# A graph attention block on one core: output projection and residual from two f16 parts, and a reordered first stage

## The chip, the cores and the metric

The kernel runs on one core of one Trainium2 chip. The metric is the time of one execution in device microseconds, lower is better; the runs' median is what is compared. One further execution was profiled, and its trace gives the views and rows below.

## The reference

Inputs are x (2048 rows of 256), an adjacency matrix adj of 2048 x 2048 integers, a node mask, h_target (2048 x 256) and the weights of one attention layer with 8 heads of 32 (H, HD) and of a feed-forward of 4 x 256:

```
h  = relu(layernorm(x))
hs = layer_norm(h; ln1) masked;  ht = layer_norm(h_target; ln1) masked
q, k, v = ht @ Wq + bq, hs @ Wk + bk, hs @ Wv + bv          # q also / sqrt(32)
logits  = q k^T per head, -1e30 where edge_mask (adj) is 0
ctx     = softmax(logits) v
ht      = ht + where(tmask, ctx @ Wo + bo, 0)               # output projection and residual
ht      = layer_norm(ht; ln2) masked
out     = x + ht + gelu(ht @ W1) @ W2
```

## The kernel before

Five engines run programs written out by hand, and semaphores order them. The name `mm` at line 469 issues nearly every matrix product, so products are told apart by their tiles.

**First stage.** Rows of x and of h_target are normed and turned (`turn_rows`), and `features` (ACT) writes them with features in partitions: sources into nT, targets of block 0 into nTq. `project(g)` makes queries (g = 0) and keys of the four source blocks (g = 1 to 4) from f32 operands, `values(i)` the values of two source tiles; `high_parts`, `low_parts`, `high_values` and `low_values` split the results into an f16 high part and the rest. SyncE (SP) copies the parts of keys and queries into place for each pair of heads (`place_k`, `place_q`, line 377), as soon as they are staged. `early_scores(e, i)` are unmasked scores of 128 targets by 1024 sources, from which DVE takes row maxima (`maxima`, L1203); the first eight pairs are one head. `shift_row` then turns the negated maxima into one more row of the queries, and five scores of the main loop (AHEAD) are made before it begins. POOL norms sources (L1416), multiplies them with the node mask (`drop_sources`, L1431), and makes two masks (L1436). `UNREAD` products (20 of them) are read by nobody.

**Main loop.** There are 32 units, a head (8) of a block of 512 targets (4): unit u is block k = u // 8 and r = u % 8. A unit has 16 steps s, one for each tile of 128 sources. In a step PE makes the masked scores of five steps ahead (4 mask products and one of 512 columns) into one of two banks, half a pair of early scores for two units ahead, and the context of the current tile: 8 products of 65 columns from the f16 or bf16 high part of the exponential and its f16 low part. ACT makes the exponential (L888). The low part, `prob_lo`, is a subtraction: of 16 in a unit DVE makes 4 (L1211) and POOL 12 (L1412), in units with r = 5 three and 13. Eight slots hold the parts. ACT copies the context out once per unit (L910).

Extra work stands at steps given by tables of (r, s): for block k + 1 `turn_targets` and `query_features` (QT_AT), `queries` (QP_AT), in f32; for block k - 1 sums of the context's halves (POOL, SUM_AT), norms (ACT, NORM_AT, four steps of two small copies each), `turn_context` and `context_T` (CT_AT), and the out rows (WO_AT). Two weights of the feed-forward are split in eight pieces, high parts on ACT (`weight_high`, step 6, L972), low parts on POOL (`weight_low`, step 12, L1453).

**The out row** (`out_row`, PE): for 128 targets the turned context times Wo in f32, and the turned target features times an identity in f32, both added up in a half of the bank aux:

```python
for c in range(DC):
    mm(dst, cT[:, c, t * P:(t + 1) * P], wo[:, c, :], c == 0, False, skip_group_check=True)
for c in range(DC):
    last = mm(dst[:, c * P:(c + 1) * P], nTq[:, k % 2, c, t * P:(t + 1) * P], ident32[:, :], False,
              c == DC - 1, skip_group_check=True)
```

Blocks 0 to 2 have theirs at r = 2, steps 11 and 12, and r = 3, steps 1 and 2 of the next block. `rows_out` (ACT) copies them out two by two.

**End.** After the loop the feed-forward runs block by block from f16 parts (`up_products`, `gelus` and their split, `down_products`), with the last block's context turned after f = 5 and 7 of block 0 and its four out rows after f = 2 and 4 of block 1.

## Time and profile before

| | |
|---|---|
| runs | 692.8 us median of 3 (689.97, 692.81, 692.8) |
| the profiled execution | 694.41 us, its span 692.6 us, mean granted clock 0.993 |
| busy, share of the span | PE 95%, DVE 82%, POOL 76%, ACT 70% |
| instructions | 20346, of them 8346 matrix products |
| DMA | 36.23 MB, mean 52 GB/s |
| parts of the span | first stage to 70.9 us, main loop to 593.3, the rest to 692.6 |

A product's busy time on PE contains its latency, and products overlap, so PE's work is read from start to start. The chain of work that ended last goes back only through the last few per cent of the span, so it says little here; the stages were read from the timeline, from the waits and from stretches of the span.

### The profile page before, as it was taken

Reading aid. Unit: us, or ns where it says so; the run is one execution under the profiler, and the core shown is the slowest. Engines: PE = TensorE matmul, PEld = TensorE weight load, DVE = VectorE, ACT = ScalarE, POOL = GpSimd, SP = SyncE. Lnnn points to the kernel's source line nnn. Section 1 sums busy time; section 2 is a strip of 40 time slices with the busy share of each in tenths; the row PEclk is TensorE's granted clock in tenths of the full one; section 3 lists DMA queues with packets and bytes.
Section 4 is the critical chain, followed back from the end, with each engine's and each line's share of the span. In section 5 each row is a group of like instructions: output and inputs, shape, how many; then the busy total and the mean of one; then the engine's idle time right before and its main releaser. Section 6 shows DMA issues by size and latency. Waiting matters only on the chain. (4 is left out here: it accounts for less than half of the span.)

```text
span 692.6 us, 20346 instructions
## 1 busy us (share of the span) xinstructions
PE 657.6 (95%) x8346; PEld 473.0 (68%) x8346; DVE 569.2 (82%) x946; ACT 484.0 (70%) x932; POOL 524.2 (76%) x488
## 2 busy tenths in 40 slices
PE   4898999999999999999999999999999899899998
PEld 4465667766776777677767766777777567557767
DVE  5987899989999879999997798989868888575661
ACT  4865668766778858677787686778866788867550
POOL 3574889889999957899998678999977777471430
PEclk9998999999999999999999999999999999999999
DMA  8735501113001011220011112012000000000001
GB/s 296 258 80 153 177 31 36 59 63 108 2 2 34 2 62 63 58 82 2 2 33 33 62 33 78 17 51 74 2 2 2 2 3 2 1 1 32 24 17 54
DMA packets 20797, 36.23 MB, mean 52 GB/s; under 512 B 2752, under 2 KB 13280, under 8 KB 20704
## 3 DMA queue, kind: packets, MB, share of 16 engines
q1 hardware_dynamic: 20704, 34.92, 16.2%
q8 instruction: 66, 1.08, 0.6%
q14 instruction: 27, 0.22, 0.1%
HBM read 26.49 MB, written 2.10 MB: 41 GB/s over the span
## 5 line engine op out<-in xcount | busy, mean ns | idle before, releaser
L1412 POOL TENSOR_TENSOR prob_lo<-prob 128x512 f16<-128x512 f32 x382 | 437.1, 1169 | 74.1 <-ACT prob L888 73.2
L888 ACT ACTIVATE prob<-score 128x512 f32<-128x512 f32 x512 | 304.1, 597 | 135.8 <-PE score L469 128.3
L469 PE MATMUL score<-nidentb,mask_nat 128*128 128x128 bf16 x2048 | 199.1, 220 | 4.1 <-ACT qT L905 1.9
L469 PE MATMUL early<-kT,qT 96*128 96x512 f16 x512 | 192.9, 382 | 10.5 <-DVE half_max L1203 10.1
L469 PEld LDWEIGHTS ctx<-v_sb,prob 128*128 128x128 bf16 x2048 | 159.0, 98 | 60.2 <-ACT raw L910 12.6
L469 PE MATMUL score<-qT,kT 97*128 97x512 f16 x512 | 196.3, 383 | 0.0
L1203 DVE CUSTOM_DVE_ANT_0 early<-early,mask_nat,half_max 128x1024 f32<-128x1024 f32 x128 | 163.6, 1287 | 38.0 <-PE early L469 36.0
L469 PE MATMUL ctx<-v_sb,prob 128*128 128x65 f16 x2048 | 191.4, 193 | 2.3 <-ACT raw L910 1.8
L469 PE MATMUL ctx<-v_sb,prob_lo 128*128 128x65 f16 x2048 | 190.4, 193 | 0.0
L469 PEld LDWEIGHTS ctx<-v_sb,prob_lo 128*128 128x128 f16 x2048 | 142.6, 97 | 49.9 <-issue 4.0
L1203 DVE CUSTOM_DVE_ANT_0 early<-early,mask_nat 128x1024 f32<-128x1024 f32 x128 | 157.1, 1229 | 22.5 <-PE early L469 20.8
L1211 DVE TENSOR_TENSOR prob_lo<-prob 128x512 f16<-128x512 f32 x130 | 127.8, 984 | 4.1 <-ACT prob L888 4.0
L469 PEld LDWEIGHTS score<-nidentb,mask_nat 128*128 128x128 bf16 x2048 | 122.6, 98 | 8.9 <-ACT prob L888 3.2
L469 PEld LDWEIGHTS early<-kT,qT 96*128 96x128 f16 x512 | 50.6, 99 | 21.4 <-DVE half_max L1203 18.4
L469 PEld LDWEIGHTS score<-qT,kT 97*128 97x128 f16 x512 | 50.3, 98 | 0.0
L1509 POOL TENSOR_TENSOR mask_nat<-mask_nat,tgt 128x256 f32<-128x256 f32 x16 | 15.3, 965 | 44.9 <-DVE mask_nat L1355 44.9
L1341 DVE TENSOR_TENSOR kT<-qT,kT 128x512 f16<-128x512 f32 x32 | 27.3, 859 | 20.5 <-ACT kT L1081 20.5
L469 PE MATMUL early<-w_f,kT 128*128 128x256 f16 x384 | 42.7, 273 | 0.7 <-DVE adj_in L1364 0.7
L469 PEld LDWEIGHTS early<-w_f,kT 128*128 128x128 f16 x384 | 37.4, 98 | 6.1 <-DVE adj_in L1364 1.2
L1203 DVE DVE_READ_ACCUMULATOR2_ANT half_max<- 128x1 f32 x256 | 35.5, 139 | 0.0
L1077 ACT ACTIVATE qT<-score 128x512 f32<-128x512 f32 x32 | 19.0, 593 | 19.4 <-PE score L469 14.9
L1191 DVE TENSOR_SCALAR mask_nat<-adj_in 128x1024 bf16<-128x1024 int32 x26 | 26.3, 1016 | 0.0
(167 smaller groups left out, 623.2 us busy)
## 6 DMA issues: line engine op xcount, KB each, us to landing
adj_in<-in_adj SPq DMA_DIRECT2D x26, 512.0 KB, 4.0
qT<-q_stage SPq DMA_DIRECT2D x48, 64.0 KB, 2.0
kT<-mask_nat SPq DMA_DIRECT2D x48, 64.0 KB, 2.0
raw<-in_x SPq DMA_DIRECT2D x4, 512.0 KB, 5.6
tgt<-in_L_gnn_h_target SPq DMA_DIRECT2D x4, 512.0 KB, 11.6
prob<-in_adj SPq DMA_DIRECT2D x4, 512.0 KB, 10.4
nT<-in_L_gnn_W SPq DMA_DIRECT2D x2, 1024.0 KB, 6.6
mask_nat<-in_x SPq DMA_DIRECT2D x1, 2048.0 KB, 8.3
```

Source lines behind the costliest of these rows:

```text
L469: return nc.tensor.matmul(dst, w, m, start=start, stop=stop, **more)
L888: nc.scalar.activation(prob[:, n % SLOTS, :], score[n % 2][:, :], ACT.Exp).then_inc(exp_done, 1)
L1077: nc.scalar.activation(gelu[:, f % 2, :], up[f % 2][:, :], ACT.Gelu_apprx_tanh).then_inc(gelu_ready, 1)
L1191: nc.vector.tensor_scalar(mask_half(k, i), adj_home(k, i), 0.0, BIG, ALU.is_equal, ALU.mult).then_inc(mask_dve, 1)
L1203: nc.vector.tensor_tensor_reduce(out=early[e % 2][:, :], in0=early[e % 2][:, :], in1=mask_nat[:, k % 2, t, half * HALF:(half + 1) * HALF], ...
L1211: nc.vector.tensor_tensor(prob_lo[:, n % SLOTS, :], prob[:, n % SLOTS, :], prob_hi(n % SLOTS), ALU.subtract).then_inc(lo_sem["dve"], 1)
L1341: nc.vector.tensor_tensor(g_lo[:, k % 2, f, :], gelu[:, f % 2, :], g_hi[:, k % 2, f, :], ALU.subtract).then_inc(g_lo_done, 1)
L1412: nc.gpsimd.tensor_tensor(prob_lo[:, n % SLOTS, :], prob[:, n % SLOTS, :], prob_hi(n % SLOTS), ALU.subtract).then_inc(lo_sem["pool"], 1)
L1509: nc.gpsimd.tensor_tensor(xin[:, n - 1, :], xin[:, n - 1, :], tgt[:, n - 1, :], ALU.add).then_inc(r_done, 1)
```

## The change

The out rows take f16 parts: context, Wo and target features are each a high and a low f16 part, Wo needs three products where there was one in f32 (high x high, high x low, low x high), and the residual two. ACT makes the high parts as copies to f16: Wo once (unit 3, step 2), the features of a block at the steps T_HIGH, the context one step after its copy out. POOL makes the low parts as f32 minus f16 to f16: `output_low`, `feature_low`, `context_low`, at its steps WO_LOW, T_LOW and C_LOW. The parts of the context lie in cT, those of the features in nTq; the f32 forms lie in q_stage (context), in the second half of nTq (features of block 0) and in cT (features of blocks 1 to 3). The first pair of out rows moves from step 11 to 12. In the first stage 24 unread products come in (UNREAD_LATER), `project(2)` and `project(3)` are halved around `turn_rows`, two pairs of early scores come ahead of `project(4)`, `values(2)` to `values(7)` follow the early scores of the same number, `shift_row(0)` goes ahead of the tenth pair, and the orders of ACT, DVE and POOL are written anew.

```diff
-WIDE, UNREAD = 64, 20
+WIDE, UNREAD, UNREAD_LATER = 64, 20, 24
...
-WO_AT = {(2, 11): 0, (3, 1): 1}
+WO_AT = {(2, 12): 0, (3, 1): 1}
...
+T_HIGH = {0: [(3, 7), (3, 9)], 1: [(4, 6), (4, 8)]}
+T_LOW = {0: [(3, 12), (3, 15)], 1: [(4, 11), (4, 14)]}
+C_LOW = [(2, 10), (2, 12)]
+WO_HIGH, WO_LOW = (3, 2), (4, 5)
...
+        t_full = [nTq[:, 1, :, :], cT[:, :, :], cT[:, :, :], cT[:, :, :]]
+
+        t_parts = [nTq[:, i, :, :].rearrange("p c t -> p (c t)").bitcast(F16).rearrange("p (r c t) -> p r c t", r=2, c=DC)
+                   for i in range(2)]
+        c_full = [cnorm[:, :, c * P:(c + 1) * P] for c in range(DC)]
+        c_parts = cT[:, :, :].rearrange("p c t -> p (c t)").bitcast(F16).rearrange("p (r c t) -> p r c t", r=2, c=DC)
...
+                    if t == 0:
+                        pe.wait_ge(wo_lo, 1)
+                        pe.wait_ge(c_lo, DC * (k + 1))
+                        pe.wait_ge(t_lo, DC * (k + 1))
                     dst = aux[:, t % 2 * D:(t % 2 + 1) * D]
+                    part = slice(t * P, (t + 1) * P)
                     for c in range(DC):
-                        mm(dst, cT[:, c, t * P:(t + 1) * P], wo[:, c, :], c == 0, False, skip_group_check=True)
+                        for a, w in ((0, 0), (0, 1), (1, 0)):
+                            mm(dst, c_parts[:, a, c, part], wo_parts[:, w, c, :], c == a == w == 0, False, skip_group_check=True)
                     for c in range(DC):
-                        last = mm(dst[:, c * P:(c + 1) * P], nTq[:, k % 2, c, t * P:(t + 1) * P], ident32[:, :], False,
-                                  c == DC - 1, skip_group_check=True)
+                        for a in range(2):
+                            last = mm(dst[:, c * P:(c + 1) * P], t_parts[k % 2][:, a, c, part], ident16[:, :], False,
+                                      c == DC - 1 and a == 1, skip_group_check=True)
...
                 values(0)
+                for i in range(UNREAD_LATER):
+                    mm(early[1][:, TB:TB + P], identb[:, :], identb[:, :], True, True)
+                project(2, (0,))
                 turn_rows(3)
-                project(2)
+                project(2, (1,))
                 values(1)
+                project(3, (0,))
                 turn_rows(4)
-                project(3)
-                values(2)
-                for i in range(2):
-                    early_scores(0, i)
-                project(4)
-                for e in range(1, RAMP + 2):
+                project(3, (1,))
+                for e in range(2):
                     for i in range(2):
                         early_scores(e, i)
-                    if e + 2 < NT // 2:
-                        values(e + 2)
-                shift_row(0)
+                project(4)
+                for e in range(2, RAMP + 2):
+                    if e == RAMP + 1:
+                        shift_row(0)
+                    for i in range(2):
+                        early_scores(e, i)
+                    if e < NT // 2:
+                        values(e)
...
+                    nc.scalar.activation(c_full[c], aux[:, :].rearrange("p (t q) -> p t q", t=TT), ACT.Copy).then_inc(aux_done, 1)
...
+                def context_high(k, c):
+                    act.wait_ge(aux_done, AUX["cT", k, c] + 1)
+                    if c == 0 and k + 1 < NTB:
+
+                        act.wait_ge(t_lo, DC * (k + 2))
+                    nc.scalar.activation(c_parts[:, 0, c, :].rearrange("p (t q) -> p t q", t=TT), c_full[c], ACT.Copy).then_inc(c_hi, 1)
...
+                    affine(t_full[k][:, c, :], aux[:, :], LN1_G[:, c:c + 1], RES_B[:, c:c + 1]).then_inc(aux_done, 1)
...
+                def feature_high(k, c):
+                    if k == 0:
+                        act.wait_ge(nT_done, c + 1)
+                    else:
+                        act.wait_ge(aux_done, AUX["qT", k, c] + 1)
+                    if c == 0:
...
+                    nc.scalar.activation(t_parts[k % 2][:, 0, c, :], t_full[k][:, c, :], ACT.Copy).then_inc(t_hi, 1)
+
+                def output_high():
+                    nc.scalar.activation(wo_parts[:, 0, :, :], wo[:, :, :], ACT.Copy).then_inc(wo_hi, 1)
...
+                features(2)
                 deviation(2)
...
-                features(2)
+                high_values(0)
                 deviation(3)
-                last_sources()
-                high_values(0)
...
+                last_sources()
...
                 high_parts(3)
+                high_parts(4)
+                high_values(2)
+                feature_sum(0)
+                feature_sum(1)
+                for i in range(3, 6):
+                    high_values(i)
                 for k in range(1, 3):
                     target_deviation(k)
                 nc.scalar.activation(warm_c, eps_c, ACT.Exp).then_inc(act_link, 1)
-                high_values(2)
-                high_parts(4)
-                feature_sum(0)
-                high_values(3)
-                high_values(4)
-                feature_sum(1)
-                for i in range(5, NT // 2):
-                    high_values(i)
+                high_values(6)
                 negated(0)
                 row_out(0)
+                high_values(7)
...
+                        if k == 0 and (r, s) in T_HIGH[0]:
+                            feature_high(0, T_HIGH[0].index((r, s)))
+                        if k + 1 < NTB and (r, s) in T_HIGH[1]:
+                            feature_high(k + 1, T_HIGH[1].index((r, s)))
+                        if (u, s) == WO_HIGH:
+                            output_high()
...
+                            if (r, s - 2) in CT_AT:
+                                context_high(k - 1, CT_AT[r, s - 2])
...
+                        context_high(NTB - 1, f // 2 - 2)
...
+                low_parts(0)
...
-                low_parts(0)
                 low_parts(1)
                 low_values(0)
+                make_mask(0, 0)
+                low_parts(2)
+                for i in range(1, TT):
+                    make_mask(0, i)
+                low_values(1)
+                low_parts(3)
+                maxima(0)
+                maxima(1)
+                low_parts(4)
+                maxima(2)
+                low_values(2)
+                make_mask(0, 4)
+                maxima(3)
+                make_mask(0, 5)
                 target_stats(1)
-                low_parts(2)
+                maxima(4)
                 target_stats(2)
-                low_values(1)
-                for i in range(2):
-                    make_mask(0, i)
-                low_parts(3)
-                for i in range(2, TT):
-                    make_mask(0, i)
-                maxima(0)
-                low_values(2)
-                low_parts(4)
-                maxima(1)
-                make_mask(0, 4)
-                maxima(2)
-                make_mask(0, 5)
-                for e in range(3, RAMP + 1):
+                for e in range(5, RAMP + 2):
                     maxima(e)
-                for e in range(RAMP + 1, RAMP + FILL):
+                for e in range(RAMP + 2, RAMP + FILL):
                     maxima(e)
...
+                def output_low():
+                    pool.wait_ge(wo_hi, 1)
+                    nc.gpsimd.tensor_tensor(wo_parts[:, 1, :, :], wo[:, :, :], wo_parts[:, 0, :, :], ALU.subtract).then_inc(wo_lo, 1)
+
...
+                    parts = t_parts[k % 2]
+                    nc.gpsimd.tensor_tensor(parts[:, 1, c, :], t_full[k][:, c, :], parts[:, 0, c, :], ALU.subtract).then_inc(t_lo, 1)
...
+                def context_low(k, c):
+                    pool.wait_ge(c_hi, DC * k + c + 1)
+                    hi, lo = (c_parts[:, i, c, :].rearrange("p (t q) -> p t q", t=TT) for i in range(2))
+                    nc.gpsimd.tensor_tensor(lo, c_full[c], hi, ALU.subtract).then_inc(c_lo, 1)
...
                 source_norm(1)
+                drop_sources(1)
                 source_norm(2)
-                drop_sources(1)
...
+                        if k == 0 and (r, m) in T_LOW[0]:
+                            feature_low(0, T_LOW[0].index((r, m)))
+                        if k + 1 < NTB and (r, m) in T_LOW[1]:
+                            feature_low(k + 1, T_LOW[1].index((r, m)))
+                        if k > 0 and (r, m) in C_LOW:
+                            context_low(k - 1, C_LOW.index((r, m)))
+                        if (u, m) == WO_LOW:
+                            output_low()
...
+                for c in range(DC):
+                    context_low(NTB - 1, c)
```

How it moves instructions, on PE in the first stage from the values of the first tiles to the first scores (mask_nat and raw are sources, cT holds the weights of keys and values here, kT and qT make the early scores). Before:

```order
L469 MATMUL early<-cT,nT 128x256 x4
L483 MATMUL score<-ident,raw 128x128 x8
L469 MATMUL ctx<-nT,cT 128x512 x2
L469 MATMUL aux<-nT,cT 128x512 x2
L469 MATMUL early<-cT,nT 128x256 x4
L483 MATMUL score<-ident,raw 128x128 x8
L469 MATMUL ctx<-nT,cT 128x512 x2
L469 MATMUL aux<-nT,cT 128x512 x2
L469 MATMUL score<-cT,nT 128x256 x4
L469 MATMUL early<-kT,qT 128x512 x2
L469 MATMUL ctx<-nT,cT 128x512 x2
L469 MATMUL aux<-nT,cT 128x512 x2
```

And now:

```order
L485 MATMUL early<-cT,nT 128x256 x4
L485 MATMUL early<-identb 128x128 x24
L485 MATMUL ctx<-nT,cT 128x512 x2
L499 MATMUL score<-ident,raw 128x128 x8
L485 MATMUL aux<-nT,cT 128x512 x2
L485 MATMUL early<-cT,nT 128x256 x4
L485 MATMUL ctx<-nT,cT 128x512 x2
L499 MATMUL score<-ident,raw 128x128 x8
L485 MATMUL aux<-nT,cT 128x512 x2
L485 MATMUL early<-kT,qT 128x512 x4
L485 MATMUL ctx<-nT,cT 128x512 x2
L485 MATMUL aux<-nT,cT 128x512 x2
```

The 24 products on identb are new, the two key projections after them are cut in halves of two products, and four early products stand ahead of the last key projection.

On POOL from the loop's start to the middle of block 0 (prob_lo is the loop's own subtraction, w_f the weights' low part). Before:

```order
L1412 TENSOR_TENSOR prob_lo<-prob 128x512 x60
L1453 TENSOR_TENSOR w_f<-nT,w_f 128x512
L1412 TENSOR_TENSOR prob_lo<-prob 128x512 x13
L1453 TENSOR_TENSOR w_f<-nT,w_f 128x512
L1412 TENSOR_TENSOR prob_lo<-prob 128x512 x12
L1453 TENSOR_TENSOR w_f<-nT,w_f 128x512
L1412 TENSOR_TENSOR prob_lo<-prob 128x512 x12
L1453 TENSOR_TENSOR w_f<-nT,w_f 128x512
```

And now:

```order
L1474 TENSOR_TENSOR prob_lo<-prob 128x512 x48
L1524 TENSOR_TENSOR nTq<-nTq 128x512
L1474 TENSOR_TENSOR prob_lo<-prob 128x512 x2
L1524 TENSOR_TENSOR nTq<-nTq 128x512
L1474 TENSOR_TENSOR prob_lo<-prob 128x512 x5
L1519 TENSOR_TENSOR wo_parts<-wo,wo_parts 128x512
L1474 TENSOR_TENSOR prob_lo<-prob 128x512 x4
L1524 TENSOR_TENSOR nTq<-cT,nTq 128x512
L1474 TENSOR_TENSOR prob_lo<-prob 128x512
L1515 TENSOR_TENSOR w_f<-nT,w_f 128x512
L1474 TENSOR_TENSOR prob_lo<-prob 128x512
L1524 TENSOR_TENSOR nTq<-cT,nTq 128x512
```

Five subtractions of 128x512 come in among them: the features' of block 0 and of block 1 (nTq) and Wo's. Those of cT stand further down, two in each block from the second on, among the subtractions of unit r = 2.

On PE, one pair of out rows in unit 10, with the steps around it left out. Before:

```order
L469 MATMUL score<-qT,kT 128x512
L469 MATMUL early<-kT,qT 128x512
L469 MATMUL aux<-wo,cT 128x256 x2
L469 MATMUL aux<-ident,nTq 128x128 x2
L469 MATMUL ctx<-v_sb,prob 128x65
```

And now:

```order
L485 MATMUL score<-qT,kT 128x512
L485 MATMUL early<-kT,qT 128x512
L485 MATMUL aux<-wo_parts,cT 128x256 x6
L485 MATMUL aux<-ident,nTq 128x128 x4
L485 MATMUL ctx<-v_sb,prob 128x65
```

The products on wo are six f16 ones for two f32 ones (each of which the chip runs as two instructions), those on nTq four for two.

## Rows read from the trace of the kernel before

**Rows 1.** The page's first part: busy time, share of the span, instructions.

```profile
PE 657.6 (95%) x8346; PEld 473.0 (68%) x8346; DVE 569.2 (82%) x946; ACT 484.0 (70%) x932; POOL 524.2 (76%) x488
```

**Rows 2.** Timeline, PE, a plain step (start, us, engine, line, operation, out<-in, shape, count).

```profile
300.59 0.39 PE L469 MATMUL score<-nidentb,mask_nat 128*128 128x128 bf16 x4
300.81 0.38 PE L469 MATMUL score<-qT,kT 97*128 97x512 f16 x1
301.03 0.38 PE L469 MATMUL early<-kT,qT 96*128 96x512 f16 x1
...
301.49 0.39 PE L469 MATMUL score<-nidentb,mask_nat 128*128 128x128 bf16 x4
```

**Rows 3.** Timeline, ACT, 319 to 351: the context copies of units 14 to 16.

```profile
319.69 0.39 ACT L910 ACTIVATE raw<-ctx 128x260 f32<-128x260 f32 x1
...
334.59 0.39 ACT L910 ACTIVATE raw<-ctx 128x260 f32<-128x260 f32 x1
...
349.77 0.39 ACT L910 ACTIVATE raw<-ctx 128x260 f32<-128x260 f32 x1
```

**Rows 4.** Waits: who waited for whom, us in total, times, longest.

```profile
ACT prob L888 <- PE score L469: 128.3, 290, 1.6
```

**Rows 5.** Stretches: us, busy us (instructions) of PE, PEld, DVE, ACT, POOL, PE's clock, DMA.

```profile
127.00:161.00 34.00, 33.47 (x470) 23.42 (x467) 30.42 (x46) 23.89 (x44) 29.36 (x25) 1.00 0.21 63
161.00:200.30 39.30, 39.20 (x602) 28.56 (x600) 36.91 (x54) 28.97 (x54) 39.17 (x34) 1.00 0.12 36
277.00:300.00 23.00, 21.66 (x309) 15.12 (x307) 21.06 (x32) 16.57 (x33) 19.86 (x17) 1.00 0.26 72
```

**Rows 6.** Stretches, the same columns: units 10 and 19.

```profile
231.40:250.20 18.80, 18.57 (x260) 14.45 (x257) 17.07 (x30) 13.16 (x28) 13.14 (x13) 1.00 0.09 30
384.30:403.20 18.90, 18.53 (x259) 14.44 (x255) 16.05 (x27) 12.49 (x24) 13.94 (x13) 1.00 0.18 57
```

**Rows 7.** Timeline, PE: one out row and what follows it.

```profile
243.64 1.03 PE L469 MATMUL aux<-wo,cT 128*128 128x256 f32 x4
...
244.95 0.19 PE L469 MATMUL ctx<-v_sb,prob 128*128 128x65 f16 x1
```

**Rows 8.** Groups: line, engine, operation, out<-in, shapes, count, busy us, mean ns, idle before.

```profile
L972 ACT ACTIVATE w_f<-nT 128x512 f16<-128x512 f32 x8 | 5.0, 621 | 0.0
...
L1453 POOL TENSOR_TENSOR w_f<-nT,w_f 128x512 f16<-128x512 f32 x8 | 11.0, 1378 | 0.0
...
L1126 DVE BATCH_NORM_STATS2 st_t<-tgt 128x6 f32<-128x256 f32 x12 | 4.2, 411 | 0.0
...
L1129 DVE BATCH_NORM_AGGREGATE mv_t<-st_t 128x2 f32<-128x6 f32 x12 | 1.1, 158 | 0.1
```

**Rows 9.** Timeline, PE: the down product of block 0.

```profile
625.19 10.71 PE L469 MATMUL early<-w_f,kT 128*128 128x256 f16 x96
```

**Rows 10.** Timeline, POOL: a low part beside DVE's, and one alone.

```profile
149.87 1.49 POOL L1412 TENSOR_TENSOR prob_lo<-prob 128x512 f16<-128x512 f32 x1
...
152.31 1.04 POOL L1412 TENSOR_TENSOR prob_lo<-prob 128x512 f16<-128x512 f32 x1
```

**Rows 11.** Stretches, columns as in rows 5: at the lower granted clock.

```profile
31.73:35.10 3.37, 3.37 (x4) 1.31 (x5) 3.34 (x8) 2.64 (x5) 1.32 (x2) 0.50 0.18 43
62.45:69.28 6.83, 5.92 (x29) 3.48 (x30) 3.94 (x8) 2.60 (x5) 2.20 (x3) 0.50 0.39 95
```

**Rows 12.** Timeline, DVE: the first and the ninth maximum.

```profile
46.76 1.23 DVE L1203 CUSTOM_DVE_ANT_0 early<-early,mask_nat 128x1024 f32<-128x1024 f32 x1 [0.18 <-DVE mask_nat L1191]
...
62.48 1.26 DVE L1203 CUSTOM_DVE_ANT_0 early<-early,mask_nat 128x1024 f32<-128x1024 f32 x1
```

**Rows 13.** Timeline, PE, first stage: projection of block 1, shift row, ramp's end.

```profile
31.64 3.65 PE L469 MATMUL ctx<-nT,cT 128*128 128x512 f32 x4 [1.19 <-POOL nT L1431]
...
63.50 0.63 PE L469 MATMUL aux<-ident,shift 128*97 128x128 f16 x4
...
70.91 0.39 PE L469 MATMUL score<-nidentb,mask_nat 128*128 128x128 bf16 x4
```

More of the change, by code:

```diff
@@ L194, in gnn_kernel @@
         wo = sb("wo", [P, DC, D], F32)
+        wo_parts = sb("wo_parts", [P, 2, DC, D], F16)
         ident32 = sb("ident32", [P, P], F32)
@@ L228, in gnn_kernel @@
         big_c, eps_c, warm_c = (big[:, i:i + 1] for i in range(3))
+        node_r, vec_r, node_rows = (q_stage[0:NT, :, :, :].rearrange("p r c t -> p (r c t)").bitcast(F32)[:, i * P:(i + 1) * P]
+                                    for i in range(3))
+        node_i = node_rows.bitcast(I32)
         src = raw[:, :, :].rearrange("p k c -> p (k c)")[:, 0:NT * D].rearrange("p (t d) -> p t d", d=D)
@@ L484, in turn_rows, with project @@
                         last.then_inc(tp_ready, 1)
-                def project(g):
+                def project(g, halves=range(DC)):
                     what = GROUPS[g]
@@ L495, in project @@
                         pe.wait_ge(bc_done, 1)
-                    for m in range(DC):
+                    for m in halves:
                         if g == 0 and m == 1:
@@ L504, in project @@
                             w = wq[:, c, m * P:(m + 1) * P] if what == "t0" else wkv[:, 0, c, m * P:(m + 1) * P]
-                            r = nTq[:, 0, c, :] if what == "t0" else nT[:, what, c, :]
+                            r = t_full[0][:, c, :] if what == "t0" else nT[:, what, c, :]
                             last = mm(proj_bank(g, m), w, r, c == 0, c == DC - 1)
@@ L649, in queries @@
                         aux_free(("qp", k, m))
-                    last = mm(aux[:, :], wq[:, c, m * P:(m + 1) * P], nTq[:, k % 2, c, :], c == 0, c == DC - 1)
+                    last = mm(aux[:, :], wq[:, c, m * P:(m + 1) * P], t_full[k][:, c, :], c == 0, c == DC - 1)
                     if c == DC - 1:
@@ L932, in context_T @@
                     job_here("cT", k, c)
-                    nc.scalar.activation(cT[:, c, :], aux[:, :], ACT.Copy).then_inc(aux_done, 1)
+                    nc.scalar.activation(c_full[c], aux[:, :].rearrange("p (t q) -> p t q", t=TT), ACT.Copy).then_inc(aux_done, 1)
[4 more added lines that the diff above has]
+                    nc.scalar.activation(c_parts[:, 0, c, :].rearrange("p (t q) -> p t q", t=TT), c_full[c], ACT.Copy).then_inc(c_hi, 1)
                 def rows_out(k, i):
```

17 lines of the change are left out of this document (10 added, 7 removed).

## Prediction

> **What bounds the kernel now.** I read the page first. TensorE (PE) is busy for 95% of the span [rows 1], but a matmul's busy time contains its latency, so I went to the timeline and took start to start. In a plain step (one tile of 128 sources for one head) 4 mask products of 128 columns start at 300.59 and the next form at 300.81, so a 128-column product costs 55 ns, and the 512-column score product after it 0.22 us; the next step's mask products start at 301.49: a plain step is 0.90 us of gapless PE work, and 16 of them with their shift row are one unit (one head of one block) [rows 2]. The starts of ScalarE's context copy, one per unit, lie 14.90 us apart [rows 3]. Plain units are bound by PE. Those with extra work (r = 2, 3, 4 of a block) last 18 to 20 us, and it is PE that is added to there.
>
> The others have little room. ScalarE (ACT) waited 128.3 us for scores, 0.25 us per step [rows 4]. GpSimd (POOL) is full between 161 and 200 us (39.17 of 39.30) and has 4.6 us idle in the 34 us before that [rows 5]. VectorE (DVE) had 1.7 of 18.8 us idle in unit 10 and 2.85 of 18.9 in unit 19 [rows 6]; I count about 1.2 of that as handovers that can't be filled.
>
> **Part 1: the out rows on PE.** An out row is 4 f32 products of 256 columns and 4 of 128 columns, 243.64 to 244.95: 1.31 us [rows 7]. With four blocks of four there are 16, 21.0 us in all. Now there are 6 f16 products of 256 columns and 4 of 128. The first kind stands in the down product: 96 of them in 10.71 us, less a latency at the end, 110 ns each [rows 9]; the second is the 55 ns of the mask products [rows 2]. That is 0.66 + 0.22 = 0.88 us, 0.43 less: **-5.2 us for the 12 out rows of the loop, -1.7 for the 4 after it**.
>
> The Trainium skill speaks against the 55 ns: its page TensorE: Matmul & The Clock Gate, section Back-to-back issue gap, has a stream of weight load and matmul pairs at about 81 ns for 128 columns. By it the 64 residual products would cost 1.7 us more, an estimate from that page. The trace's 55 ns, with a weight load each, disagrees, and the sum keeps it.
>
> PE gets its time back only where nobody else is late. Each heavy unit loses 0.87 us of PE time. Beyond its handovers DVE has 0.5 us in unit 10, with the last block's statistics, and 1.6 in unit 19. Unit 10 comes out 0.4 short; for three blocks I give back 1.0, between 0 and 2.6 (half of the 5.2). **Loop: -4.2.**
>
> **Part 2: the high parts on ACT.** 15 copies of 128x512 f32 to f16 stand in the loop (8 of features, 6 of the context, 1 of the weights), 0.62 us each as the weights' high parts [rows 8]. Lower end 0; upper end what one step's idle time leaves, 0.62 - 0.25 = 0.37 each, 5.6 us. The nearest row is nearly the same load: in the first unit of a block the context norms put two small copies into each of four steps running, and that unit lasts 15.18 instead of 14.90 us [rows 3], 0.07 per step. 15 x 0.07 is 1.0; (3, 7), (3, 9) and (4, 6) share their steps or their neighbours with a row copy, a negation or a weights' high part: 0.4 more. **+1.4.** What queues behind a copy is the next exponential, and PE waits for that with two score banks only.
>
> **Part 3: the low parts on POOL.** 17 subtractions. The weights' low parts, of the same shape, took 1.38 us in the mean [rows 8]. Block 0 gets five in units 3 and 4: 5 x 1.38 = 6.9 us against 4.6 idle before 161, and POOL is full behind that [rows 5]. So 2.3 are left over; a context product waits for its low part, and PE stops. The lead of five steps and eight slots hides some: **+1.4**, between 0 and 3. In blocks 1 and 2 the two feature parts, 2.8 us, meet 3.1 us idle between 277 and 300 [rows 5], and the two context parts 5.7 us idle in unit 10 and 5 in unit 19 [rows 6]: nothing. The context's low parts come after POOL's steps 10 and 12, and POOL runs some four steps ahead of PE's context, so they are done before the first out row, now at step 12: no wait.
>
> **Part 4: the first stage.** Before, PE waits 1.19 us ahead of 31.64 [rows 13] and then runs 3.4 us at half the granted clock, 1.2 instead of 2.4 GHz [rows 11]: 4 products take 3.65 us to their end [rows 13]. Now 24 unread products (24 x 55 ns = 1.3 us) and half a projection fill that hole, POOL masks the sources of block 1 before the next norm, and the two first early scores stand ahead of the last projection. Chained by hand from these durations, the first maximum starts near 42 instead of 46.76 [rows 12]. But DVE gets two target statistics (4.2 + 1.1 us for three, 1.8 each [rows 8]) in between the maxima. From 42 on: two maxima at 1.35, key low parts until 45.7 (they wait for ACT), a maximum, a value low part 0.7, a mask, a maximum, a mask, 1.8, a maximum, 1.8, three maxima: the eighth ends near 60, against the start of the ninth at 62.48 [rows 12]. **-2.5.** Then the shift row and the ramp's five scores: 63.50 to 70.91, 7.4 us [rows 13], nearly all at the lower clock [rows 11]. Its 20 mask products, 9 products of 512 columns and the mean are 3.9 us at the full level; 2 us of the 7.4 are the clock's. PE is denser ahead of it now, and I take three quarters: **-1.5**. Head: -4.0, between 0 (the drop comes anyway, a queue is late) and -5.
>
> **Part 5: the end.** The out rows give -1.7. Two high copies (1.2 us) come into ACT's densest stretch between the gelu copies, and POOL must split the last context before the first out row: +0.9, between 0 and 1.7. **-0.8.**
>
> Sum: -4.0 - 4.2 + 1.4 + 1.4 - 0.8 = **-6.2 us**. The profiled span 692.6 becomes 686.4. That execution was timed at 694.4, 1.6 above the runs' median of 692.8; off the median the forecast is **686.6 us**.
>
> **Rivals.**
> 1. The first stage gives nothing: SyncE's placing copies come late, or the clock falls at another point. For it: DVE's chain of eight maxima gets only 2.5 us shorter by my sum, and one queue's delay eats that. 686.6 + 4.0 = 690.6. Chance 0.15.
> 2. DVE becomes the bound in the heavy units: its idle time there [rows 6] can't be used, and PE waits for maxima. All of the loop's 4.2 goes: 690.8. Against: 2.85 us idle in unit 19. Chance 0.12.
> 3. Slower: POOL's queue is strictly in order, and 15 new subtractions stand in it between the probabilities' low parts. If its idle time lies ahead of them and can't be used behind, each costs PE its whole 1.38 us: 20.7 instead of 1.4, 706. It turns to slower from about 6 uncovered of the 15 (7.6 us are gained before POOL's term), by over 0.5% from 8. For: 39.17 of 39.30 us busy [rows 5], and a low part takes 1.49 instead of 1.04 when a DVE subtraction runs beside it [rows 10], so that each new one also meets DVE. Against: over 5 us idle in each of the units that take the context's parts [rows 6]. Chance 0.05. The Trainium skill's page SBUF — State Buffer, section Who interferes with whom, goes that way: a DVE instruction with two SBUF inputs contends with a GpSimd one that reads SBUF; the trace agrees by that 0.45 us.
> 4. A 128-column f16 product costs 80 instead of 55 ns (the page is named in part 1): 64 x 26 ns = 1.7 us, 688.3. No row here has it. Chance 0.03.
> 5. All covers hold, no stall by ACT, POOL or DVE (-1.4, -1.4, -1.0): 682.8. For it: most copies have a step to themselves. Chance 0.15.
>
> The forecast's own case has 0.50, and with its costs inside their bounds it reaches from 684 to 689.3. Rivals 5 and 4 lie at its edges or in it, 1 and 2 just above. **Range 682.5 to 691.0**: it leaves out rival 3 and the ends of 5, 1 and 2, with the scatter of runs (those before lie 2.8 us apart). A measurement of this kernel can tell about 0.5%, 3.5 us, from no change, so faster is under 689.3: nearly all of the forecast's case, 5 and 4, a little of 1 and 2: 0.70. Within 0.5%: 0.24. Slower: 0.06.
>
> **What the profile after would show.** Right: the ten products of an out row in 0.88 us, start to start; the ramp's last score before 68 us and no stretch at the lower clock after 35 us; units 10, 11, 18, 19, 26 and 27 each 0.6 to 0.9 us shorter; POOL full from about 127 us on to 200, with PE stopping once or twice before a context product in units 4 to 7; plain units still 14.9 us. Wrong: waits for maxima that grow by over 3 us in the heavy units (rival 2), the eighth maximum ending after 62 us (rival 1), units 4 to 8 longer by over 3 us together or units 10 to 13 longer at all (rival 3), 80 ns between residual products (rival 4).

## The result and the profile after

The changed kernel takes **686.71 us** (median of 5 runs, 686.42 to 687.35), against 692.81 us for the kernel before (689.97 to 693.06): a ratio of 0.992, 95% interval 0.990 to 0.994, 6.1 us less. One execution of experiment 7's kernel (1013.55 us) and one of the kernel before (1710.11) lie far outside and are left out of the ranges below. The profiled execution was timed at 686.55 us and has a span of 684.8 us. The page's first part:

```profile
PE 649.5 (95%) x8402; PEld 464.4 (68%) x8402; DVE 577.8 (84%) x946; ACT 490.3 (72%) x949; POOL 546.2 (80%) x505
```

Against [rows 1] PE (TensorE) has 8.1 us less to do, POOL (GpSimd) 22.0 more, ACT (ScalarE) 6.3 more, and DVE (VectorE) 8.6 more, though not one DVE instruction was added (946 in both). Stretches of the changed kernel, then of the one before, in the columns of [rows 5]: first stage, loop to the end of unit 30, rest.

```profile
0.00:65.70 65.70, 54.55 (x279) 36.53 (x280) 52.99 (x160) 42.69 (x77) 36.18 (x53) 1.00 0.66 208
65.70:576.00 510.30, 494.00 (x7292) 357.76 (x7291) 462.46 (x695) 384.69 (x769) 464.52 (x410) 1.00 0.13 40
576.00:684.80 108.80, 101.00 (x838) 70.16 (x834) 62.37 (x93) 62.92 (x104) 45.53 (x45) 1.00 0.06 20
```

```profile
0.00:70.90 70.90, 56.67 (x255) 37.48 (x256) 54.87 (x160) 43.36 (x77) 38.41 (x54) 0.93 0.62 194
70.90:583.20 512.30, 498.40 (x7269) 363.63 (x7268) 454.29 (x695) 378.75 (x754) 445.07 (x393) 1.00 0.13 39
583.20:692.60 109.40, 102.50 (x829) 71.86 (x825) 60.02 (x93) 61.85 (x102) 40.69 (x43) 1.00 0.06 20
```

So the first stage became 5.2 us shorter, the loop 2.0 and the rest 0.6: 7.8 us between these two executions, of which 1.6 belongs to this execution of before (timed 694.4, its median 692.8).

The same stretches as [rows 11]: the granted clock is now 1.00 (2.4 GHz) where it was 0.50.

```profile
31.73:35.10 3.37, 3.37 (x16) 2.29 (x15) 3.37 (x6) 2.98 (x5) 2.26 (x2) 1.00 0.09 22
62.45:69.28 6.83, 6.50 (x61) 3.79 (x59) 5.83 (x10) 4.91 (x10) 6.67 (x7) 1.00 0.42 104
```

An out row on PE's timeline (it was 1.31 us in [rows 7]): its ten products run from 242.45 to 243.33, 0.88 us.

```profile
242.45 0.82 PE L485 MATMUL aux<-wo_parts,cT 128*128 128x256 f16 x6
243.11 0.39 PE L485 MATMUL aux<-ident,nTq 128*128 128x128 f16 x4
243.33 0.19 PE L485 MATMUL ctx<-v_sb,prob 128*128 128x65 f16 x1
```

Right ahead of these products PE waited 0.95 us for a maximum of DVE, its only long wait in unit 10; in the kernel before it waited there for no maximum:

```profile
242.22 0.39 PE L485 MATMUL early<-kT,qT 96*128 96x512 f16 x1 [0.95 <-DVE half_max L1264]
```

ACT's context copies close a unit, as in [rows 3]. After: the copies of units 4 to 6, then 9 to 12.

```profile
149.98 0.39 ACT L938 ACTIVATE raw<-ctx 128x260 f32<-128x260 f32 x1
167.35 0.39 ACT L938 ACTIVATE raw<-ctx 128x260 f32<-128x260 f32 x1
182.25 0.39 ACT L938 ACTIVATE raw<-ctx 128x260 f32<-128x260 f32 x1
...
228.72 0.40 ACT L938 ACTIVATE raw<-ctx 128x260 f32<-128x260 f32 x1
247.93 0.40 ACT L938 ACTIVATE raw<-ctx 128x260 f32<-128x260 f32 x1
265.45 0.39 ACT L938 ACTIVATE raw<-ctx 128x260 f32<-128x260 f32 x1
285.14 0.39 ACT L938 ACTIVATE raw<-ctx 128x260 f32<-128x260 f32 x1
```

Unit 5 lasts 17.37 us, unit 6 still 14.90. The lengths of all units, by the starts of their first mask products, differ from before in these only:

```
unit      3     4     5      10     11     12     18     19     20     26     27
before  16.59 18.32 15.82  18.78  18.92  19.63  18.79  18.91  19.57  18.79  17.84
after   16.71 18.50 17.38  19.15  17.98  19.70  18.04  17.98  19.69  17.93  16.98
```

Units 11, 18, 19, 26 and 27 give 0.75 to 0.94 us each, as an out row pair should. Unit 5 gives 1.56 us back, and unit 10 is longer though PE has 0.9 us less to do in it. PE's waits (who waited for whom, us, times, longest), in the whole changed kernel, in the whole kernel before, and in the changed kernel's unit 5 alone:

```profile
PE early L485 <- DVE half_max L1264: 11.4, 17, 1.4
PE ctx L485 <- ACT raw L938: 1.7, 7, 0.3
```

```profile
PE early L469 <- DVE half_max L1203: 10.1, 15, 1.4
```

```profile
PE early L485 <- DVE half_max L1264: 1.5, 2, 1.0
PE ctx L485 <- POOL prob_lo L1474: 0.2, 1, 0.2
```

PE stops for the **maxima of DVE**, hardly for POOL, though only POOL and ACT got work. DVE's and POOL's timelines show how, around POOL's new low part of a feature half (L1524) in unit 4:

```profile
141.90 1.50 DVE L1252 TENSOR_SCALAR mask_nat<-adj_in 128x1024 bf16<-128x1024 int32 x1
143.33 1.22 DVE L1264 CUSTOM_DVE_ANT_0 early<-early,mask_nat 128x1024 f32<-128x1024 f32 x1
```

```profile
141.70 1.16 POOL L1524 TENSOR_TENSOR nTq<-cT,nTq 128x512 f16<-128x512 f32 x1
142.82 1.49 POOL L1474 TENSOR_TENSOR prob_lo<-prob 128x512 f16<-128x512 f32 x1
```

DVE's mask starts 0.2 us into POOL's subtraction, ends 0.5 us after it, and takes 1.50 us; POOL's next one then takes 1.49 instead of 1.04. The maximum, which reads a PSUM bank and a mask, isn't held: it takes its usual 1.22 beside that next one. In the kernel before, such a mask was first by 0.06 us: it took 0.69 us, and POOL's low part was the one that waited:

```profile
155.89 0.69 DVE L1191 TENSOR_SCALAR mask_nat<-adj_in 128x1024 bf16<-128x1024 int32 x1
```

```profile
155.95 1.52 POOL L1412 TENSOR_TENSOR prob_lo<-prob 128x512 f16<-128x512 f32 x1 [0.61 <-ACT prob L888]
```

In both pairs the second to start waits out the first. More subtractions in POOL's queue are more for such operations of DVE to wait for.

### The profile page after: what moved, and what is told of

Same layout as the page of the kernel before. It is cut to its first block and busy times, and to the rows that moved or that the text cites. A ratio compares the mean times of both kernels' runs of the same rounds, so it can differ in the third digit from the quotient of the medians.

```text
span 684.8 us, 20508 instructions
## 1 busy us (share of the span) xinstructions
PE 649.5 (95%) x8402; PEld 464.4 (68%) x8402; DVE 577.8 (84%) x946; ACT 490.3 (72%) x949; POOL 546.2 (80%) x505
## 5 line engine op out<-in xcount | busy, mean ns | idle before, releaser
L1272 DVE TENSOR_TENSOR prob_lo<-prob 128x512 f16<-128x512 f32 x130 | 132.0, 1017 | 4.0 <-ACT prob L916 4.0
```

The lines of the kernel that those rows point to most:

```text
L1272: nc.vector.tensor_tensor(prob_lo[:, n % SLOTS, :], prob[:, n % SLOTS, :], prob_hi(n % SLOTS), ALU.subtract).then_inc(lo_sem["dve"], 1)
```

## The experiments

The expectations were on record before each run. The clock is the mean granted one of a run. Spans of the loop and units are from each kernel's trace.

**1. The new first stage alone.** The kernel before with only the four orders of the first stage changed (PE, ACT, DVE, POOL) and the 24 unread products.

> The kernel before, with only the new order of the first stage (the halves of the key projections, the early scores of pairs 0 and 1 ahead of the last projection, the 24 further unread products, the orders of ScalarE, VectorE and GpSimd there). The two profiles place the loop's first unit 5.2 us earlier, where the prediction had 4.0. Theory 1, the first stage is a term of its own and the head's gain is carried through the loop: 687.6 to 688.6 us (692.8 less 4.2 to 5.2), the loop and the end as long as before, no lowered clock after 16 us. Rival, part of the 5.2 us is the lowered clock of this one profiled execution of before and its median has less of it: 689 to 690.5 us. Rival, the loop's first units wait longer (maxima late) and give it back: unit 0 and 1 together over 1 us longer than before.

Measured: 689.37 us (12 runs, 688.99 to 690.32), ratio 0.995 (0.993 to 0.997). In its trace the first stage is 65.6 us long and the loop and the rest are what they were before:

```profile
0.00:65.60 65.60, 53.83 (x279) 35.46 (x280) 53.16 (x160) 42.80 (x77) 36.24 (x53) 1.00 0.66 208
65.60:577.80 512.20, 498.31 (x7268) 363.57 (x7267) 454.05 (x695) 378.37 (x754) 446.35 (x395) 1.00 0.13 40
577.80:687.20 109.40, 102.53 (x830) 71.91 (x826) 60.05 (x93) 61.85 (x102) 40.69 (x43) 1.00 0.06 20
```

The first rival holds. The runs say why (us by granted clock; the 23 of before are those of this comparison):

```
clock            1.0                 0.998             0.995            0.993             0.988-0.990
before           690.01-690.19 (9)   691.50-.62 (2)    692.96-693.44(2) 694.39-694.81 (8) 696.42, 696.89
first stage new  688.99-690.32 (11)  690.11 (1)
```

Before, the granted clock differs from run to run, and the time with it, over 6.9 us. The new order has no run under 0.998. Against runs of before at the full clock it gains only 0.7 us (medians 690.07 and 689.35); the rest of the median's 3.6 us, 2.9, is clock that is no longer lost.

**2. The parts alone.** The changed kernel with the old first stage.

> The changed kernel with the old order of the first stage: only the output projection and residual from two f16 parts. Theory 1, the parts are a term of their own: the loop 2.0 us shorter and the end 0.6 us, so 690.2 us, with unit 5 at 17.4 us where before had 15.8. Rival, unit 5's delay comes from where the new first stage leaves the engines (VectorE a pair behind): then unit 5 is near 15.8 us here and the time is 688.6 us.

Measured: 689.71 us (12 runs, 687.42 to 693.45, clocks 0.990 to 1.0), ratio 0.996 (0.993 to 0.999). Unit 5 lasts 17.40 us and every other unit is as in the changed kernel, so theory 1 holds and the rival falls. At the full clock it has 687.42 and 687.61: 2.5 us under before. 0.7 and 2.5 make 3.2 of the 3.4 us that lie between the full-clock runs of both kernels (690.07 and 686.64); the two halves add up. So of the median's 6.1 us some 2.7 are clock that is no longer lost.

**3. Both kinds of parts cut.**

```diff
-nc.scalar.activation(t_parts[k % 2][:, 0, c, :], t_full[k][:, c, :], ACT.Copy).then_inc(t_hi, 1)
+nc.scalar.activation(t_parts[k % 2][:, 0, c, 0:CUT], t_full[k][:, c, 0:CUT], ACT.Copy).then_inc(t_hi, 1)
...
-nc.gpsimd.tensor_tensor(parts[:, 1, c, :], t_full[k][:, c, :], parts[:, 0, c, :], ALU.subtract).then_inc(t_lo, 1)
+nc.gpsimd.tensor_tensor(parts[:, 1, c, 0:CUT], t_full[k][:, c, 0:CUT], parts[:, 0, c, 0:CUT], ALU.subtract).then_inc(t_lo, 1)
```

CUT is 16. The context's parts are cut in the same way, PE reads a zeroed tile in their place, and the two parts of Wo stay whole. The kernel leaves these parts out of its output.

> The changed kernel, with the high and low parts of the feature blocks and of the context cut from 512 columns to 16 (ten ScalarE copies... four for the features, eight for the context's eight halves, each a few columns; the same count of GpSimd subtractions), TensorE reading zeros in their place: so the out rows' f16 products alone, nearly without the engines' new work. Output leaves these parts out. If the new work on ScalarE and GpSimd is what took the loop's gain: unit 5 at 15.8 us, unit 10 at 18.0, units 3 and 4 at their old lengths, loop 3 to 3.4 us shorter than the changed kernel's, time 683.3 to 683.8 us. If VectorE alone bounds the heavy units (the rival of the prediction): unit 10 stays over 18.7 us and the time is 684.5 to 685.5 us.

Measured: 681.90 us (681.70 to 682.09), better than either theory. Unit 5 15.82, units 3 and 4 as before; units 12 and 20, where there is no out row, fell to 18.78 and 18.77, below what they were before (19.63, 19.57): in unit 20 of the kernel before PE waits 0.8 us for a maximum, and here it doesn't. Unit 10 stayed at 19.13.

**4. Only POOL's low parts cut.** ACT's high copies stand; those of the features and the context alone lose their low parts, which the output leaves out.

> The changed kernel with only GpSimd's low parts of features and context cut to 16 columns, TensorE reading zeros for them (left out of the output); ScalarE's high copies stand. If GpSimd's full queue, or its reads beside VectorE, makes unit 5's 1.56 us and unit 10's 0.4 to 1.1: 683.8 to 684.6 us, within 0.5 us of the kernel with both cut. If ScalarE's copies make them (exponentials late): within 0.4 us of the changed kernel, 686.3 to 686.8 us, and unit 5 stays at 17.4.

Measured: 683.52 us (682.88 to 683.95), 3.2 us under the changed kernel; the GpSimd theory holds for unit 5 (15.82), not for unit 10 (19.14), and units 12 and 20 are at 18.91 and 18.77. PE's waits in the whole of it, and in its unit 5:

```profile
PE early L487 <- DVE half_max L1266: 8.5, 14, 1.4
```

```profile
PE early L487 <- DVE half_max L1266: 0.5, 1, 0.5
```

The loops of the two cut kernels, for comparison with 510.30 (changed) and 512.30 (before):

```profile
66.00:572.50 506.50, 493.37 (x7293) 357.87 (x7292) 455.40 (x695) 380.80 (x769) 449.76 (x409) 1.00 0.13 40
```

```profile
65.80:572.90 507.10, 493.81 (x7293) 358.00 (x7292) 455.59 (x695) 385.10 (x769) 449.13 (x410) 1.00 0.13 40
```

So in the loop the f16 rows alone (with Wo's parts) give 5.8 us, ACT's copies take 0.6 back, and POOL's low parts 3.2. Behind the loop the same three are 1.6, 0.7 and 0.3 us: this last part lasts 109.4 us before, 107.8 with both cut, 108.5 with the low parts cut, 108.8 changed. DVE is busy 6.9 us longer in the loop with POOL's low parts than without (462.46 to 455.59), doing the same.

**5. The first stage without the 24 unread products** (their number set to 0).

> The changed kernel without the 24 unread products of 56 ns in its first stage (1.3 us of TensorE). The runs of before come with granted clocks between 0.988 and 1.0 and lie between 690.0 and 696.9 us in that order, those of the kernel with the new first stage all at 0.998 to 1.0. Theory 1, the unread products keep TensorE at its upper clock while it would wait: without them part of the runs show a clock under 0.998 and lie 1.5 to 4 us higher, the median at 687.5 to 690 us. Rival, the new order alone leaves no gap long enough: all runs at 1.0 and the time 685.4 to 686.7 us.

Measured: 686.79 us (686.68 to 687.48), five runs at 1.0 and two at 0.998. The rival holds: they aren't what keeps the clock in the first stage, and leaving them out gains nothing. Which piece of the new order keeps it wasn't tried. The profiled run, at 0.998, has its lowered stretch elsewhere, in unit 28, which then lasts 18.62 instead of 17.86 us:

```profile
530.00:549.00 19.00, 17.23 (x234) 12.31 (x233) 15.03 (x27) 13.76 (x23) 13.74 (x13) 0.91 0.01 2
```

**6. The statistics out of unit 10.**

```diff
-if r == 2 and j < TT and k == 1:
-    next_stats(NTB - 1, j)
+if r == 3 and j < 2 and k == 1:
+    for t in (2 * j, 2 * j + 1):
+        next_stats(NTB - 1, t)
```

> The changed kernel with the statistics of the last block's target rows (four, next_stats) made by VectorE in unit 11 instead of unit 10. Unit 10 took 19.15 us, and 19.13 with all new copies cut, where unit 18, which has the same work but these statistics, took 18.04. If VectorE bounds unit 10 and nothing of the new copies: unit 10 goes to 18.0 to 18.2, unit 11 (VectorE busy 16.6 of 18.0 us) grows by 0 to 0.5, the time 685.6 to 686.2 us. If something else of unit 10 holds it (the out row moved by a step): unit 10 stays over 18.8, 686.6 to 687.2 us.

Measured: 687.37 us (687.15 to 688.18). Unit 10 went to 18.05, as said, and PE's wait for a maximum in it is gone, so VectorE bounds it; but unit 11 grew by 1.81 to 19.79, more than I had allowed.

**7. The same into unit 0:**

> The changed kernel with the four statistics of the last block's target rows moved from unit 10 to unit 0 (maxima 4 to 7), where VectorE is busy 16.44 of 17.41 us. Moving them to unit 11 gave unit 10 1.10 us and cost unit 11 1.81. If there is room in unit 0: unit 10 at 18.05, unit 0 up to 0.3 us longer, 685.4 to 685.9 us. If VectorE has no room anywhere: the 1.1 us comes back in units 0 and 1, 686.4 to 687.0 us.

Measured: 686.63 us (686.39 to 687.40). Unit 10 18.04, unit 0 unchanged, unit 1 0.90 longer (17.43), as the second theory says: PE waits there for maxima for 1.9 us, where it was 1.4. DVE has no such room in either place.

**8. The first block's low parts in unit 0** (tables T_HIGH, T_LOW of block 0: (0, 5), (0, 7) and (0, 8), (0, 12); WO_LOW (3, 12)).

> The changed kernel with the first feature block's high parts made in unit 0 (steps 5 and 7) and its low parts there too (steps 8 and 12) instead of unit 3, and the low part of the output weights at unit 3 step 12 instead of unit 4 step 5. Nothing is left out. If the crowding of GpSimd's five new subtractions into units 3 and 4 makes unit 5's 1.56 us: unit 5 goes to 15.8 to 16.3 us and the time to 685.0 to 685.7 us, with unit 0 or 1 up to 0.5 us longer. If the last two subtractions, in unit 4, do it alone: unit 5 stays at 17.4 and the time is 686.5 to 687.3 us.

Measured: 686.22 us (685.99 to 686.36). Unit 5 16.94, unit 3 16.59, the rest as it was: 0.44 of unit 5's 1.56 us went, a result between the two theories. The last two subtractions, in unit 4, keep the larger share.

**9. One source instead of two in POOL's low parts.**

```diff
-nc.gpsimd.tensor_tensor(lo, c_full[c], hi, ALU.subtract).then_inc(c_lo, 1)
+nc.gpsimd.tensor_scalar(lo, c_full[c], 0.0, None, ALU.mult).then_inc(c_lo, 1)
```

(and so for the features' low parts; the output leaves them out)

> The changed kernel, with GpSimd's fourteen... in fact sixteen low parts of features and context made by a one-source operation (times zero, so that they are left out of the output) instead of a subtraction of two sources; the operation on 128x256 took 0.54 us in the first stage, so on 128x512 it lasts as long as the subtraction, 1.05 us, and GpSimd's queue is as full. If it is GpSimd's time that delays unit 5, and units 12 and 20: 686.3 to 687.0 us, unit 5 at 17.4. If it is VectorE's operations held up while a two-source subtraction of GpSimd runs (128x8 operations of 0.16 us took 1.0 to 1.1 beside one): 683.3 to 684.3 us as with the low parts cut, unit 5 at 15.8, and no VectorE operation longer than 0.75 us beside the new ones.

Measured: 686.30 us (686.15 to 687.50), but the operation took 1.48 to 2.04 us, not 1.05 (second fence; first the changed kernel's):

```profile
L1529 POOL TENSOR_TENSOR cT<-q_stage,cT 128x512 f16<-128x512 f32 x8 | 10.4, 1300 | 12.1 <-ACT cT L968 12.1
L1524 POOL TENSOR_TENSOR nTq<-cT,nTq 128x512 f16<-128x512 f32 x6 | 7.8, 1304 | 0.0
```

```profile
L1529 POOL TENSOR_SCALAR cT<-q_stage 128x512 f16<-128x512 f32 x8 | 13.2, 1646 | 11.8 <-ACT cT L968 11.8
L1524 POOL TENSOR_SCALAR nTq<-cT 128x512 f16<-128x512 f32 x6 | 9.4, 1560 | 0.0
```

So it tells less than it should. But the trace shows that DVE is held less beside it. A low part of DVE's that starts inside a low part of POOL's, in the changed kernel and then here:

```profile
369.25 1.26 DVE L1272 TENSOR_TENSOR prob_lo<-prob 128x512 f16<-128x512 f32 x1
```

```profile
369.78 0.72 DVE L1272 TENSOR_TENSOR prob_lo<-prob 128x512 f16<-128x512 f32 x1
```

POOL's operation runs here from 369.35 for 1.49 us, so DVE's begins and ends inside it. In units 12 and 20 POOL was busy longer per part and yet they became 0.55 us shorter (19.15), which speaks for the hold. In unit 5 (17.14) PE's stop changed its cause:

```profile
PE ctx L485 <- POOL prob_lo L1474: 1.7, 3, 0.9
```

There PE waits for POOL's full queue, and for as long as it did for maxima. Unit 4 grew by 0.75, unit 9 by 0.3. So both prices occur. How unit 5's 1.56 us divide between DVE's hold and POOL's queue with subtractions of the usual length isn't shown: cutting the low parts (experiment 4) takes away both.

**10. The later low parts into plain units.** As 8, with T_LOW's further blocks at (6, 2), (7, 2).

> As the kernel with the first block's low parts in unit 0, and the further feature blocks' low parts moved from steps 11 and 14 of units 4, 12 and 20 to step 2 of units 6 and 7, 14 and 15, 22 and 23. Units 5, 12 and 20 were 1.56, 0.79 and 0.92 us shorter with the low parts cut. If the crowding makes these and a plain unit has room for one subtraction: unit 5 at 15.8, units 12 and 20 at 18.9, 683.7 to 684.5 us. If every GpSimd subtraction holds VectorE up wherever it stands: each of the six plain units grows by 0.3 to 0.8 us, 686 to 688 us.

Measured: 689.06 us (688.07 to 689.73), 2.8 slower than kernel 8. Its full-clock runs fall in two groups, 688.07 to 688.22 (5) and 689.05 to 689.29 (6), and the profiled one (688.17) is of the lower: between the two traces lie 1.9 us. Unit 5 15.83 and unit 12 18.91, as hoped; unit 20 only went to 19.62 instead of 18.8, and PE waits 0.8 us for a maximum in it as in the kernel before, though no new subtraction stands there. So its length with low parts (19.69) isn't the price of these subtractions alone. And units 6, 7, 8, 9 grew by 0.59, 1.19, 0.26, 0.31, and 14 to 17 by the same; in 22 and 23 it was only 0.06 and 0.09. The slower theory holds for 6, 7, 14 and 15. Units 6, 7, 14 and 15 also hold a low part of the weights; 22 and 23 don't. PE's waits in units 6 and 7 (164.7 to 196.2):

```profile
PE ctx L485 <- POOL prob_lo L1474: 1.1, 3, 0.4
```

**11. The later low parts a unit earlier** (as 8; T_HIGH (3, 9), (3, 15), T_LOW (3, 12), (4, 1)).

> As the kernel with the first block's low parts in unit 0, and the further feature blocks' low parts moved from steps 11 and 14 of units 4, 12 and 20 to step 12 of the unit before and step 1 of these (their high parts to steps 9 and 15 of the unit before). VectorE is busy 16.6 of 18.0 us in unit 11, GpSimd 13.4. If what counts is that the subtraction stands in a unit whose VectorE has room: units 12 and 20 at 18.9 to 19.3, unit 11 as before, unit 5 at 15.8 to 16.3, 684.0 to 685.2 us. If unit 4's own crowding stays (its first subtraction at step 1): unit 4 or 5 over 0.8 us longer than with the parts cut, 685.2 to 686.5 us.

Measured: 688.15 us (687.27 to 688.95), 1.9 slower than kernel 8. Unit 5 15.83, but unit 3 17.83 (+1.24), unit 4 +0.25, 11 and 19 +0.45, 12 and 20 at 20.06 and 20.00. Both theories were too low.

**12. The weights' parts out of the way.** As 8, and:

```diff
-HIGH_AT = [3, 4, 5, 6, 7, 12, 13, 14]
-LOW_AT = [4, 5, 6, 7, 13, 14, 15, 21]
+HIGH_AT = [5, 6, 7, 12, 13, 14, 15, 21]
+LOW_AT = [6, 7, 13, 14, 15, 21, 22, 23]
```

> As the kernel with the first block's low parts in unit 0, and the eight parts of the up and down weights moved out of the units where the new subtractions stand: ScalarE's high parts from units 3, 4, 5, 6, 7, 12, 13, 14 to 5, 6, 7, 12, 13, 14, 15, 21, GpSimd's low parts from units 4, 5, 6, 7, 13, 14, 15, 21 to 6, 7, 13, 14, 15, 21, 22, 23. Nothing is left out. If GpSimd's count in units 4 and 5 (the two feature subtractions, and two of the weights') makes the rest of unit 5's delay: unit 5 from 16.94 to 15.8 to 16.1 us, the other units as they were, 684.9 to 685.5 us. If the two feature subtractions of unit 4 make it alone: unit 5 stays at 16.9 and the time at 686.0 to 686.5 us.

Measured: **684.40 us** (683.68 to 685.71), ratio 0.990 (0.986 to 0.993) to before, 2.3 under the changed kernel's median with nothing left out. Unit 5 16.30 (0.64 less than in 8, not the whole), units 3 and 4 0.2 less each, unit 9 0.3. Unit 1 is 0.9 shorter, as in kernel 10 too, though neither kernel differs from kernel 8 up to there, so it isn't the edit's doing. PE's wait for a maximum in it is 0.5 us here and 1.4 in the changed kernel; what sets it is open. Since executions of one kernel can lie 0.9 us apart at the full clock (experiment 10), up to 0.9 of the 2.3 us may be chance; units 3, 4, 5 and 9 together are 1.9 us shorter than in the changed kernel. Its profiled run loses 0.7 us in unit 28 to a lowered clock, as in 5.

## Why the prediction was right, and where only its sum was

The forecast was 686.6 us, and 686.71 came out. Step by step:

**Part 1, an out row in 0.88 us:** exact, 242.45 to 243.33; products of 256 columns 110 ns, of 128 columns 55 ns. The 81 ns of the Trainium skill's page TensorE: Matmul & The Clock Gate, section Back-to-back issue gap, don't appear; rival 4 is out. The loop's gain, -4.2 with DVE's give-back of 1.0, was mis-sized: by experiment 3 the rows alone give 5.8, more than PE's own 5.2, since units 12 and 20 drop by 0.8 as well, each by one wait for a maximum. The give-back was right in kind for unit 10 (VectorE with the last block's statistics, experiments 6 and 7); it is 1.2 us there, the 0.9 not gained and 0.37 on top, and nothing in units 18 and 26.

**Part 2, ACT +1.4:** measured 0.6 in the loop (506.5 to 507.1, without Wo's copy, which stands in both). What was wrong is 0.07 per copy for all copies: units 26 and 27 show none, units 3, 4, 12 and 18 0.1 to 0.2 each.

**Part 3, POOL +1.4:** measured 3.2. The size in block 0 was near (unit 5, 1.56), the mechanism was not. I wrote that "a context product waits for its low part, and PE stops"; PE stopped for maxima instead (1.5 us in unit 5, against 0.2 for low parts), since masks and low parts of DVE, which stand ahead of the maxima, are held while a subtraction of POOL runs. And "nothing" for blocks 1 and 2 was wrong: without the low parts units 12 and 20 are 0.8 and 0.9 shorter. I had compared POOL's new work with POOL's idle time, and never priced what it does to DVE. Rival 3 had the contention, but priced it on POOL's side only (1.04 to 1.49). The Trainium skill's page SBUF — State Buffer, section Who interferes with whom, says that the order of issue, and not the operation's shape, decides which of the two engines blocks; the traces agree by DVE's mask, 1.50 us when it starts second and 0.69 when it starts first.

**Part 4, the first stage -4.0:** measured 5.2 between the profiled executions, and 3.6 between medians (experiment 1). But the split was wrong. "-2.5" for the maxima and "-1.5" for the clock should have been about -0.7 and the rest, by the full-clock runs of experiment 1. The eighth maximum does end at 59.8, as forecast, and the ninth starts here:

```profile
60.48 1.23 DVE L1264 CUSTOM_DVE_ANT_0 early<-early,mask_nat 128x1024 f32<-128x1024 f32 x1 [0.59 <-PE early L485]
```

instead of 62.48 [rows 12]; but most of those 2 us were the clock's as well. The first lowered stretch [rows 11] lay ahead of the maxima and delayed them, and I had counted only the second as the clock's. I also took one execution's clock for the kernel's: its runs range over six levels, 0.988 to 1.0. Rival 1 is out for the median, though at the full clock the first stage gives only 0.7 us; the ramp's last score starts at 64.67, before the 68 I had set, and the loop at 65.75.

**Part 5, the end -0.8:** measured -0.6, and its terms were near: the rows -1.6 for -1.7, the copies and low parts +1.0 for +0.9 (experiment 4).

**The sum:** first stage 1.2 us more gain than forecast, loop 0.6 more, end 0.2 less; less 1.6 us by which I had set the profiled execution off from the median. In the median it is 6.1 against 6.2. That it hits within 0.1 us is luck. Three errors in the loop (rows +1.6, POOL -1.8, ACT +0.8) nearly cancel. And the working started from the profiled execution, where the change brought 7.8 us and not 6.2; in the medians this doesn't show, since the median execution of before was 1.6 us faster than the profiled one. POOL is full from 127 to 200 us, as said (33.78 of 34.00 and 39.30 of 39.30). Units 10 and 12 grew by 0.37 and 0.07, which I had named as a sign of rival 3. Unit 10 isn't POOL's doing: it is as long with the low parts cut (experiment 4), and experiment 6 shows that the statistics bound it. Why it is longer than before, which had the same statistics, is open. Rival 2's mark, 3 us more waits for maxima, was not reached: 1.3.

## What to carry to other kernels

Work given to an idle engine can be paid by that engine's neighbours too: before costing a GpSimd subtraction at "its idle time", look at how long the VectorE operations beside such subtractions already take, and whether VectorE has the room. Look for what shares the same units and can be moved (here the weights' parts, which had no due time before the loop's end) before moving what has due times. And where a profile shows a stretch at the lower clock, ask several executions whether they all have it: a change that closes a gap may gain its clock in the runs that lost it, and next to nothing in the others.

## What the runs showed of the hardware that was not expected

- A VectorE operation that reads two tensors in SBUF waits out the GpSimd subtraction that is running, however small it is: the product of 128x4 elements (L1311) took 164 to 922 ns, the three-operand one after it up to 1087. So does the mask (0.69 and 1.50 us), which reads one. Statistics (L1182), which read one tensor, aren't held: 12 of the 20 started inside a GpSimd subtraction with over 0.4 us of it left, and none took over 424 ns:

```profile
L1311 DVE TENSOR_TENSOR col_l<-col_l,node_f x4: 164/907/922, 274.3 to 625.7; 128x4 f32<-128x4 f32 x4
L1312 DVE SCALAR_TENSOR_TENSOR col_l<-mv_l,col_l x4: 162/1024/1087, 275.2 to 625.9; 128x4 f32<-128x4 f32 x3, 128x8 f32<-128x8 f32 x1
L1182 DVE BATCH_NORM_STATS2 st_l<-tgt x20: 393/418/424, 231.6 to 624.5; 128x6 f32<-128x256 f32 x20
```

- Beside GpSimd's one-source multiplication VectorE's low part took 0.72 us inside it, where beside the subtraction it took 1.26 (experiment 9).
- That multiplication took 1.48 to 2.04 us on 128x512 with f16 output; a one-source multiply and add on 128x256 in the first stage, with f32 output, 0.55 in the median: more than twice that for twice the columns. What of it is the output's type wasn't tried.
- The same kernel, with nothing changed, was granted mean clocks from 0.988 to 1.0, and its time followed, 690.0 to 696.9 us (the comparison of experiment 1).
- A stretch at the lower clock also came in the middle of the loop (unit 28, in the traces of experiments 5, 7 and 12), with PE busy 19.8 of the 20 us right before it in experiment 5's; it cost 0.7 to 0.8 us. Why there is open.
